# The expert layer's first bias: from a VectorE addition to one more TensorE product per tile

## What is computed

```python
for g in range(G):
    h = jax.nn.gelu(jnp.einsum('nd,edm->enm', xf, W1[g]) + b1[g][:, None, :], approximate=False)
    o = jnp.einsum('enm,emd->end', h, W2[g]) + b2[g][:, None, :]
    y = y + jnp.einsum('end,ne->nd', o, combine[:, g, :])
```

## Time and profile before

| what | us |
|---|---|
| median of three runs | 1765.45 |
| lowest, highest | 1761.12, 1771.79 |
| the profiled execution's own time | 1771.83 |
| its span | 1770.1 |
| TensorE matmul busy | 1444.1 (82%) |
| VectorE busy | 1172.3 (66%) |
| ScalarE busy | 635.9 (36%) |
| GpSimd busy | 507.9 (29%) |

### The profile page before, as it was taken

One profiled execution on the slowest core, in us unless ns is written; L12 is line 12 of the kernel. 1 busy time (PEld: TensorE's weight loads), 2 busy tenths in 40 slices (PEclk: granted clock), 3 DMA queues, 4 the chain that ended last, 5 costly groups with the idle time before them and its releaser, 6 DMA issues. The chain is left out here.

```text
span 1770.1 us, 30141 instructions
## 1 busy us (share of the span) xinstructions
PE 1444.1 (82%) x7693; PEld 1182.5 (67%) x7704; DVE 1172.3 (66%) x1815; ACT 635.9 (36%) x833; POOL 507.9 (29%) x548
## 2 busy tenths in 40 slices
PE   6776757747777678989991699999999999889895
PEld 5353434525232223989981599999998989888895
DVE  5377877886999997394667545644454645675762
ACT  1210110113444443251110445544454535565550
POOL 0000000000141421222110445444554444444450
PEclk7698988976999999999995799999999999999995
DMA  3200000006111112223222977876777877998856
GB/s 147 102 26 8 15 7 7 15 15 217 70 41 69 53 38 74 76 62 92 89 89 82 318 183 208 221 161 160 181 193 197 202 177 187 235 281 217 233 100 203
DMA packets 91299, 223.49 MB, mean 126 GB/s; under 512 B 14616, under 2 KB 43544, under 8 KB 91012
## 3 DMA queue, kind: packets, MB, share of 16 engines
q1 hardware_dynamic: 68212, 142.23, 24.4%
q0 software_dynamic: 20864, 74.68, 20.2%
q10 hardware_dynamic: 2192, 6.20, 0.9%
HBM read 167.03 MB, written 56.05 MB: 126 GB/s over the span
## 5 line engine op out<-in xcount | busy, mean ns | idle before, releaser
L847 PE MATMUL ps_o<-prob,h_head 128*97 128x512 f32 (+1 forms) x480 | 194.0, 546 | 63.3 <-DVE prob L792 63.3
L1778 POOL DMA_INDIRECT sum_dram<-y,to_index x93 | 165.4, 1779 | 222.1 <-DMA sum_dram<-y,to_index 163.4
L2031 PE MATMUL ps_h<-e_hi,e_xt_hi 128*128 (+1 forms) x546 | 196.1, 359 | 8.3 <-DVE e_xt_lo L1923 5.1
L1923 DVE TENSOR_TENSOR e_xt_lo<-ps_xt,e_xt_hi 128x768 fp32r<-128x768 f32 x92 | 88.1, 958 | 171.5 <-ACT e_xt_hi L1871 168.0
L515 PE MATMUL ps_c<-one_src,one_dst 128*128 x528 | 125.4, 385 | 91.1 <-DVE one_dst L451 85.9
L847 PEld LDWEIGHTS ps_o<-prob,h_head 128*97 128x97 f32 x480 | 76.4, 171 | 180.6 <-issue 94.0
L2010 PE MATMUL ps_y<-e_hi,e_ht_hi 128*128 (+1 forms) x546 | 192.0, 352 | 2.0 <-DVE e_ht_lo L1963 2.0
L2031 PE MATMUL ps_h<-e_lo,e_xt_hi 128*128 (+1 forms) x546 | 186.1, 341 | 0.0
L2031 PE MATMUL ps_h<-e_hi,e_xt_lo 128*128 (+1 forms) x546 | 186.0, 341 | 0.0
L2010 PE MATMUL ps_y<-e_hi,e_ht_lo 128*128 (+1 forms) x546 | 185.1, 339 | 0.0
L1935 DVE TENSOR_TENSOR e_lo<-raw,e_hi (+1 forms) x192 | 178.9, 953 | 8.5 <-ACT e_hi L1879 7.4
(11 more groups left out here) (332 smaller groups left out, 3100.7 us busy)
## 6 DMA issues: line engine op xcount, KB each, us to landing
raw<-in_ew SPq DMA_DIRECT2D x192, 384.0 KB
b_all<-in_eb SPq DMA_DIRECT2D x32, 192.0 KB
al_src<-al_dram SPq DMA_DIRECT2D x1, 5120.0 KB, 14.4
w_room<-rel_dram SPq DMA_DIRECT2D x8, 640.0 KB, 4.8
row<-rel_dram SPq DMA_DIRECT2D x8, 640.0 KB, 4.7
xs<-in_x SPq DMA_DIRECT2D x1, 3840.0 KB, 17.8
x_in_t<-in_x SPq DMA_DIRECT2D x10, 384.0 KB, 3.5
sum_dram<-x SPq DMA_DIRECT2D x10, 384.0 KB, 3.9
```

The source lines that it names most:

```text
L847: turn = nc.tensor.matmul(ps_o[u][0:C1 + 1, c, 0:WID[c]], h_head[:, u, t, :], prob[:, t % 2, 512 * c:512 * c + WID[c]], start=(t == 0), st ...
L1778: nc.gpsimd.indirect_dma_start(s.sum_dram.ap(), bass.IndirectOffsetOnAxis(to_index[:, w:w + 1], 0), y[:, w, :], None, bounds_check=ROWS - ...
L1923: nc.vector.tensor_tensor(xt_lo[:, :, :].rearrange("p (b k) n -> p b (k n)", b=2), ps_x[:, :, 0:HALF], xt_hi[:, :, :].bitcast(F32).rearran ...
L2031: summed = nc.tensor.matmul(ps_h[:, 0:HID], a, b[:, bass.ds(e % 2, 1), c * HID:(c + 1) * HID] .rearrange("p o m -> p (o m)"), start=(c == ...
```

## The change

The bias is no longer added by VectorE. It is kept in two rows of one tile of 33 partitions, `b1_pair`: row 0 holds the high part and row 32 the low part, the rows between are zero. One more matmul at the end of the first layer's sum, of a tile of ones with `b1_pair`, adds both to each row of `ps_h`. ScalarE takes the gelu straight from `ps_h`. The bias is loaded as two single rows in place of 128, ScalarE rounds it once for each expert, and VectorE makes its low part on one partition. The tile that the loads go to is zeroed once, and the tile of ones filled, by GpSimd at the start of `plan_experts`; the load of the bias of expert 0 moves behind this on SP.

```diff
@@ plan_experts, GpSimd
+                nc.gpsimd.memset(s.b1_all[:, :, :], 0.0).then_inc(consts, 1)
+                nc.gpsimd.memset(s.ones[:, :].bitcast(F32), 1.0).then_inc(consts, 1)
                 nc.gpsimd.memset(before[:, :, :], 1.0).then_inc(consts, 1)
...
-                pool.wait_ge(consts, 10)
+                pool.wait_ge(consts, 12)
@@ plan_experts, SP
                 sp.dma_start(b2_all[:, :], b2).then_inc(b2_in, 16)
 
-                load_bias(sp, s, b1, 0)
...
-                sp.wait_ge(s.b1_in, 16)
-                sp.wait_ge(consts, 12)
+                sp.wait_ge(consts, 14)
+                load_bias(sp, s, b1, 0)
+                sp.wait_ge(s.b1_in, 32)
@@ plan_experts, VectorE
-                dve.wait_ge(consts, 12)
+                dve.wait_ge(consts, 14)
@@ load_bias
-    eng.dma_start(s.b1_all[:, bass.ds(e % BRING, 1), :].rearrange("p o m -> p (o m)"),
-                  b1[bass.ds(e, 1), :].broadcast_to([P, HID])).then_inc(s.b1_in, 16)
+    for row in (0, LOW_ROW):
+        eng.dma_start(s.b1_all[row:row + 1, bass.ds(e % BRING, 1), :].rearrange("p o m -> p (o m)"),
+                      b1[bass.ds(e, 1), :]).then_inc(s.b1_in, 16)
@@ run_experts, ScalarE
+                def bias(e):
+                    act.wait_ge(b1_in, 32 * e + 32)
+                    nc.scalar.activation(s.b1_pair[:, bass.ds(e % 2, 1), :], b1_all[:, bass.ds(e % BRING, 1), :],
+                                         ACT.Copy).then_inc(b1_hi_made, 1)
...
                     if head and not last:
                         if not start:
                             act.wait_ge(h_summed, k)
+                        bias(e + 1)
                         weights(e + 1, 0)
-                    act.wait_ge(biased, k + 1)
+                    act.wait_ge(h_summed, k + 1)
                     if not start:
                         act.wait_ge(h_turned, k)
-                    nc.scalar.activation(h_act[:, :], h_in[:, :], ACT.Gelu).then_inc(gelued, 1)
+                    nc.scalar.activation(h_act[:, :], ps_h[:, 0:HID], ACT.Gelu).then_inc(gelued, 1)
@@ run_experts, VectorE
+                def bias_rest(e):
+                    low = slice(LOW_ROW, LOW_ROW + 1)
+                    u = bass.ds(e % 2, 1)
+                    dve.wait_ge(b1_hi_made, e + 1)
+                    nc.vector.tensor_tensor(s.b1_pair[low, u, :], b1_all[low, bass.ds(e % BRING, 1), :],
+                                            s.b1_pair[low, u, :].bitcast(F32), ALU.subtract).then_inc(b1_lo_made, 1)
...
                     if head and not last:
+                        bias_rest(e + 1)
                         weights(e + 1, 0, (0, 1))
-                    dve.wait_ge(h_summed, k + 1)
-                    if head:
-                        dve.wait_ge(b1_in, 16 * e + 16)
-                    if not start:
-                        dve.wait_ge(gelued, k)
-                    nc.vector.tensor_tensor(h_in[:, :], ps_h[:, 0:HID],
-                                            b1_all[:, bass.ds(e % BRING, 1), :].rearrange("p o m -> p (o m)"),
-                                            ALU.add).then_inc(biased, 1)
@@ run_experts, TensorE
                     if not start:
-                        pe.wait_ge(biased, k)
+                        pe.wait_ge(gelued, k)
...
-                                                      start=(c == 0 and n == 0), stop=(c == KD - 1 and n == 2))
+                                                      start=(c == 0 and n == 0), stop=False)
+                    if head:
+                        pe.wait_ge(b1_lo_made, e + 1)
+                    summed = nc.tensor.matmul(ps_h[:, 0:HID], s.ones[:, :],
+                                              s.b1_pair[:, bass.ds(e % 2, 1), :].rearrange("p o m -> p (o m)"),
+                                              start=False, stop=True)
                     summed.then_inc(h_summed, 1)
@@ program
-            s.b1_all = sb("b1_all", [P, BRING, HID], where=routing)
+            s.b1_all = sb("b1_all", [LOW_ROW + 1, BRING, HID], where=routing)
+            s.b1_pair = sb("b1_pair", [LOW_ROW + 1, 2, HID], F32R, where=routing)
+            s.ones = sb("b1_ones", [LOW_ROW + 1, P], F32R, where=routing)
```

More of the change, by code:

```diff
@@ L50 @@
 BRING = 8
+LOW_ROW = 32
 SLOPE = 0.2
@@ L1663, in run_experts @@
         xt_hi, xt_lo = sb("e_xt_hi", [P, KD, P], F32R), sb("e_xt_lo", [P, KD, P], F32R)
-        h_in = sb("h_in", [P, HID])
         h_act = sb("h_act", [P, HID])
@@ L1680, in run_experts @@
         gathered, turned, x_hi_made, x_lo_made = sem("gathered"), sem("x_turned"), sem("x_hi"), sem("x_lo")
-        h_summed, biased, gelued, h_turned = sem("h_summed_2"), sem("biased"), sem("gelued"), sem("h_turned")
+        h_summed, gelued, h_turned = sem("h_summed_2"), sem("gelued"), sem("h_turned")
+        b1_hi_made, b1_lo_made = sem("e_b1_hi"), sem("e_b1_lo")
         h_hi_made, h_lo_made, y_summed, y_made = sem("h_hi"), sem("h_lo"), sem("y_summed"), sem("y_made")
@@ L1728, in load @@
                     landed = 16 * e
+                    biases = 32 * e
                     if freed is not None:
@@ L1731, in load @@
                         landed = sp.snap(loads)
+                        sp.reg_mov(rows_of, 32 * e)
+                        biases = sp.snap(rows_of)
                     sp.wait_ge(b1_in, 16)
-                    sp.wait_ge(b1_in, landed)
+                    sp.wait_ge(b1_in, biases)
                     load_bias(sp, s, b1, e)
@@ L1748, in _ @@
                 loads = sp.alloc_register("loads")
+                rows_of = sp.alloc_register("bias_rows")
                 splits = sp.alloc_register("splits")
@@ L1756, in _ @@
                     sp.wait_ge(w2_in[piece], 16 * E)
-                sp.wait_ge(b1_in, 16 * E)
+                sp.wait_ge(b1_in, 32 * E)
             @block.gpsimd
@@ L1912, in _ @@
                 act.wait_ge(ready, 1)
+                bias(0)
                 weights(0, 0)
@@ L1985, in _ @@
                 match_rows(nc, s, AHEAD - 1).then_inc(rows_made, 1)
+                bias_rest(0)
                 weights(0, 0, range(3))
```

## The result

The changed kernel takes **1790.44 us** (median of four runs, 1787.51 to 1794.38), the kernel before 1766.14 beside it. The ratio is 1.0133, with a 95% interval of 1.0106 to 1.016: slower by 1.3%, and outside the predicted range of 1758 to 1780 us.

What follows compares the result with a forecast made beforehand. TensorE was taken to bound the expert part; 15.7 - 4.5 + 2.8 - 2.2 - 1.5 - 2.7 - 4.4 = +3.2 us on the median of 1765.45 gave 1768.7 us, range 1758 to 1780 us.

Steps and rivals of the forecast that it cites:

- The added matmul: TensorE, end of the first layer's sum: 91 matmuls at 0.173 us each add 15.7 us.
- Absorbed and loads: TensorE's gather waits: 4.5 us off as 26 waits absorb the matmul, 4.4 us off from smaller bias loads.
- The half price: Bias loads ahead of gathers: each of 13 late gathers gains 0.34 us, half of a load's 0.68, being on another queue.
- The second rival: Gathers bound the late waits: each of 26 comes 0.68 us earlier, 17.7 us in place of 4.4, 1756 us; chance 0.09.
- The fills: Start of plan_experts: two GpSimd fills ahead of VectorE's first wait add 2.8 us, all on the path.
- SP: nothing: SP's load of expert 0's bias comes later, behind weights and fills, but is first read in run_experts: no cost.
- VectorE: Head tiles: without the addition, e_xt_lo and keep come 0.5 us earlier; 2.2 us off e_xt_lo waits, 1.5 off list waits.
- ScalarE: "Nothing": Head tiles: ScalarE's added bias copy, some 0.52 us per expert, is covered by 1.62 us of idle time; no cost.
- The fourth rival: ScalarE is late: its copy pushes e_xt_hi in each head tile, 16 us more, 1785 us; chance 0.04.
- Clock: TensorE behind three long list waits: waits 0.5 us shorter let the granted clock hold, 2.7 us off.
- First rival, "TensorE pays in full": 65 tiles without gather wait pay 11.2 us, loads and clock give no relief; +10.3 us, 1775.8 us; chance 0.28.
- The GpSimd rival: Head tiles: VectorE's new subtraction holds up GpSimd's gate copies, up to 2.8 us where gathers are late, 1771.5 us; chance 0.08.

Runs made afterwards that it cites:

- e3: The changed kernel with the 33-row bias matmul run twice in a row, so the bias is added twice; 1803.1 us, one run.
- e13: The changed kernel with b1_all, b1_pair and the tile of ones on 64 partitions in place of 33; 1792.0 us, one run.
- e5: The changed kernel with b1_all, b1_pair and the tile of ones on 65 partitions in place of 33; 1761.9 us, one run.
- e1: The changed kernel with b1_all, b1_pair and the tile of ones on 128 partitions, the added rows zero; 1764.6 us, ratio 0.9981 to the kernel before.
- e2: The changed kernel without the added matmul, so the bias is missing from its result; 1756.8 us, ratio 0.9939 to the kernel before.
- e7: The kernel before, with the bias loaded as two rows into a zeroed tile and VectorE's addition kept; 1748.7 us, ratio 0.9906.
- e6: e2 with the 192 KB broadcast load of the bias back in place of the two rows; 1772.2 us, ratio 1.0034 to the kernel before.
- e12: The same kernel as e5, timed again with more runs; 1766.1 us, ratio 0.999 to the kernel before.
- e9: e5 with ScalarE's bias copy moved behind e_xt_hi and VectorE's bias subtraction behind one_row; 1759.3 us, ratio 0.9962 to the kernel before.
- e10: e9 with GpSimd's two fills moved behind its other work in plan_experts; 1760.9 us, ratio 0.9962 to the kernel before.
- e11: e10 with the bias matmul at the head of the first layer's sum, not its tail; 1754.6 us, ratio 0.9927 to the kernel before.

## Why the prediction was wrong, point by point

- **The added matmul: the step that failed.** "I take 0.173, since it stands in the same stream with the same kind of addresses; 0.16 is the lower bound." It cost 0.58 us. I gave a lower bound and no upper one, and chose the nearest rows by their size: the 32-row matmuls of `finish` stand among their like the earlier trace rows, so their steps hold no change of size, and e3, and e13 against e5, show that the change is what costs. 91 x 0.58 is 53 us in place of 15.7. The prediction named 0.2 us as the point from which it is wrong; its second sign, gather waits below 8 us, came too (1.6). With 65 or 128 rows the term is right (0.17 to 0.18), and with it the ratios 0.9981 and 0.999: no change, as forecast, if 4 to 7 us below the forecast's +3.2 us. That this comes so near is in part luck. In e1 the gather waits fell by 16.6 us where the two terms for them said 8.9; the waits for lists and `e_xt_lo` fell by 0.5 where I said 3.7, and three first layers still ran at the lower clock, where I said 2.7 us off.
- **Absorbed and loads.** I said 4.5 and 4.4 us off. The 33-row matmul took 9.3 us out of the gather waits (10.9 in e2, 1.6 after), the 128-row one 3.4 (7.5 in e1). The loads are worth about 19 by e7 and 15 by e2 and e6, near my upper bound of 17.7 (26 x 0.68). The half price was argued from the two queues; the Trainium skill ("DMA: Bandwidth & Descriptors", Queues, rings and completion order) has the engines take turns between queues, and by it I had said half is the most. Measured are 0.61 us for each of 32 loads by e7, 0.45 at the low end of its interval, where half would be 0.34: so the program loses more than half of the bias load's time. By e2 and e6 it is 0.48, less clear of noise. Why is open; I ran nothing on the order within the queues. The second rival had this mechanism right, at a chance of 0.09, and it needed the small price of the matmul to show in the time.
- **How it sums.** For the 88 tiles: matmul 88 x 0.58 = +51.0; the delay of the transposes by late gathers, taken from their starts over the usual 0.175, 27.6 to 3.1, -24.5; lists -1.4; `e_xt_lo` -3.3; two fewer tiles at the lower clock (first layer 4.62 in place of 3.05 us) -3.1. That is +18.7, measured +15.9; 2.8 us stay unexplained. Against e2 the longer tiles hid 20.7 us of their price of 51.0 in waits (the gap is 30.3).
- **The fills** 2.75, said 2.8: right. "SP: nothing" held.
- **VectorE** (-2.2 and -1.5). The chain was read rightly, its relief was not. What failed is "it stands ahead of the pieces, where VectorE waits for ScalarE's pieces anyway": in the tiles that count VectorE waits for none of them in e12, nor did it before in the tile of the earlier trace rows (three pieces in 2.81 us), and the subtraction costs in full what the addition had cost. e1 and e2 keep list waits of 1.75 to 1.98 us; only e9 and the two versions built on it show 1.5 in a tile of 7.7 us or less. In the changed kernel the waits did shrink, with the longer tile.
- **ScalarE: "Nothing"** held for the most part. Its copy of 0.52 us stands ahead of the pieces too, but where `e_xt_lo` is late VectorE comes to the pieces later than ScalarE. The 1.2 us in e2's other head tiles are the only price that shows. The fourth rival had it at `e_xt_hi`, which wasn't late.
- **Clock.** Said: with a shorter wait the three long waits keep their clock, 2.7 us. Three of before's 88 tiles have a first layer at the lower clock, one of after's: from 1570 to 1575 us the granted clock is 0.66 there, behind a list wait of 1.52 us. The sign agrees, but the length of the wait isn't what decides: all of these waits are 1.52 or 1.53 us in e10 and in e11 too, and one such layer stands behind them in e10, four in e11. That two of three kept the clock in the changed kernel was luck as far as this argument goes.
- **First rival, "TensorE pays in full"**, 1775.8 us: on the right side in time, as the fourth, 1785 us, was, but not what happened, since relief by loads was large and the price was another. The GpSimd rival did not show: of 92 copies of `gate` in the changed kernel two ran beside the subtraction, 0.76 us together.

## What to carry to other kernels

A matmul priced from rows needs rows in the same company: in a stream of full matmuls, compare one of another size at its two ends too, and where it has 64 rows or fewer, try padding with zeros to 65 or more. A load that repeats one row over 128 partitions counts by all its bytes, and where gathers are late that was the largest term. When an instruction goes from a chain that somebody waits for, look at what comes into its place: 384 values on one partition cost VectorE the same 0.55 us as 384 on 128. Give the new one a place behind what others wait for, or in time that every tile spends anyway.

## What the runs showed of the hardware that I had not expected

- Going from matmuls of 128 rows to one of 33 or 64 and back costs 0.4 us more than staying (8.08 against 7.68 us per tile), and each load of weights at such a step starts with its own matmul, 0.18 to 0.25 us of idle time ahead of it. With 65 rows there is nothing of it. The price is shown, the mechanism behind it isn't. The load itself takes about the same, 0.18 us for 33 rows, 0.19 for 128. The Trainium skill ("TensorE: Matmul & The Clock Gate", Part 3: Packing small matmuls — row/col tiling) says that TensorE pulls a load of weights ahead of running matmuls where it goes to another group of rows or to the spare weight buffer. Between matmuls of one size the trace agrees; at the change of size it doesn't.
- Three VectorE casts beside a GpSimd fill of 2.66 us took 2.6 to 2.75 us each in place of 0.15 to 0.19, and ended 0.2 us after it; the second and third may only have stood behind the first. The Trainium skill ("SBUF — State Buffer", SBUF: two separate sides) has one pair of ports that GpSimd and a VectorE instruction in a two-port mode share, and whichever starts first holds it for the whole instruction; these rows agree with it (the fill starts at 932.71, the first cast at 932.80).
- A GpSimd fill of 33 x 3072 took 2.65 us, and one of 65 x 3072 took 2.66: the time goes by the values per partition. So it does on VectorE: 0.55 us for 1 x 384 as for 128 x 384.
- The gelu straight from PSUM takes 0.49 us, 0.52 from SBUF.
